# Attention over 16 heads: the products of probabilities and v issued in pairs, in the second and fourth quarter of a step

## The reference

```
# first layer: no mask
attn = softmax(q @ k.T / sqrt(16)) ; out = attn @ v        # 16 heads of 16
x    = layernorm(x + out @ Wo.T + bo)
# second layer: rotary q and k, causal mask, then a mixture of 8 experts (top 2)
h    = x + attention(rmsnorm(x, g1))
x    = layernorm(x + h + moe(rmsnorm(h, g2)))
```

## Time and profile before

| | |
|---|---|
| median of 3 runs | 1528.28 us (1528.12 to 1532.54) |
| profiled execution | 1529.67 us |
| its span, first to last instruction | 1527.9 us |
| granted TensorE clock, mean | 0.923 |
| busy: TensorE, VectorE, ScalarE, GpSimd | 84%, 63%, 54%, 46% of the span |
| `weigh` (L878): 2048 matmuls, busy | 237.2 us |
| attention stage | about 101 to 890 us of the span |

### The profile page before, as it was taken

How to read it: one execution, slowest core, us unless ns; L and a number is a source line. 1 busy time by engine, 2 the same in 40 slices (tenths; PEclk the granted TensorE clock), 3 DMA queues, 4 the chain that set the end, 5 groups by cost and what they waited for, 6 DMA issues and landing times. The chain is left out here.

```text
span 1527.9 us, 33404 instructions
## 1 busy us (share of the span) xinstructions
PE 1283.7 (84%) x11533; PEld 710.7 (47%) x11534; DVE 968.6 (63%) x1778; ACT 829.9 (54%) x1669; POOL 698.7 (46%) x717
## 2 busy tenths in 40 slices
PE   1799999999999999999999831499999999999910
PEld 0222232223223444444443311388888888888810
DVE  6478888888897888787877317443444434444446
ACT  3148888888878777666666620143443334443313
POOL 2324374546455756666564442524443344433312
PEclk9779999999999999999998865599999999999965
DMA  4417576766675878678666438292111111111136
GB/s 122 83 40 169 160 171 177 193 172 180 178 183 170 232 219 222 198 186 225 205 176 163 147 123 238 54 324 70 45 45 45 41 43 46 45 45 41 39 119 222
DMA packets 162442, 212.23 MB, mean 139 GB/s; under 512 B 28576, under 2 KB 124320, under 8 KB 162336
## 3 DMA queue, kind: packets, MB, share of 16 engines
q1 hardware_dynamic: 154848, 190.38, 45.2%
q0 software_dynamic: 7488, 20.46, 4.4%
HBM read 119.55 MB, written 82.58 MB: 132 GB/s over the span
## 5 line engine op out<-in xcount | busy, mean ns | idle before, releaser
L982 ACT ACTIVATE a_probs<-a_ps_s 128x512 f32<-128x512 f32 (+2 forms) x896 | 460.1, 569 | 172.6 <-PE a_ps_s L777 167.3
L1051 DVE TENSOR_REDUCE a_shift_max<-a_ps_m 128x1 f16<-128x512 f32 x512 | 320.7, 684 | 71.0 <-PE a_ps_m L782 69.7
L782 PE MATMUL a_ps_m<-a_qkx 48*128 48x128 f16 (+3 forms) x1408 | 287.0, 304 | 16.9 <-DVE a_shift_max L1051 8.4
L1568 PE MATMUL e_ps_gu<-e_xT,w_up 128*128 128x256 f16 x2574 | 298.1, 274 | 1.5 <-ACT e_xT L1623 1.4
L777 PE MATMUL a_ps_s<-a_qkx 49*128 49x128 f16 (+3 forms) x1408 | 277.9, 298 | 16.5 <-ACT a_probs L982 14.9
L1568 PEld LDWEIGHTS e_ps_gu<-e_xT,w_up 128*128 x2574 | 249.6, 98 | 35.0 <-issue 5.4
L878 PE MATMUL a_ps_o<-a_probs,a_v_one 128*32 128x512 f32 (+3 forms) x2048 | 237.2, 537 | 2.8 <-ACT a_o L989 2.7
L777 PEld LDWEIGHTS a_ps_s<-a_qkx 49*128 49x128 f16 x1408 | 90.7, 95 | 272.8 <-ACT a_probs L982 156.4
L1530 POOL DMA_INDIRECT y<-e_y,e_put x78 | 77.1, 988 | 250.0 <-DVE e_y L1657 238.1
L1668 DVE TENSOR_TENSOR e_h<-e_gate,e_ps_gu 128x512 f32<-128x512 f32 (+2 forms) x156 | 82.7, 551 | 136.8 <-ACT e_gate L1631 119.0
L1590 PE MATMUL e_ps_y<-w_down,e_h 128*128 x1404 | 162.7, 273 | 7.7 <-issue 5.2
(11 more groups left out here) (191 smaller groups left out, 1617.8 us busy)
## 6 DMA issues: line engine op xcount, KB each, us to landing
a_qkx<-a_qk_dram SPq DMA_DIRECT2D x192, 128.0 KB, 4.3
a_qk_dram<-a_qk SPq DMA_DIRECT2D x32, 512.0 KB, 5.5
a_o_dram<-a_o SPq DMA_DIRECT2D x64, 256.0 KB, 2.7
a_o_half<-a_o_dram SPq DMA_DIRECT2D x32, 256.0 KB
a_inv_half<-a_inv_dram SPq DMA_DIRECT2D x32, 256.0 KB
part<-a_part SPq DMA_DIRECT2D x16, 512.0 KB, 5.7
a_q_swap<-a_q SPq DMA_DIRECT2D x64, 128.0 KB, 3.9
c_rows<-y SPq DMA_DIRECT2D x16, 512.0 KB, 5.4
```

The lines of the kernel that those rows point to most:

```text
L782: return pe.matmul(out, qx[first:first + 48, r, pair, q * P:(q + 1) * P], kx[first:first + 48, r, pair, k0:k1], start=start, stop=stop)
L982: act.activation(dst, src, ACT.Exp).then_inc(exp_out, 1)
L1051: vector.tensor_reduce(out, src, AX.X, ALU.max, negate=True).then_inc(max_out, 1)
L1568: mm = pe.matmul(ps_gu[:, bank, kind, f % 2], w[:, ds(e, 1)].rearrange("p o f -> p (o f)"), xT[:, s, xh, k, :], start=n == 0, stop=n == 5)
```

## The change

In place of one `weigh` at the end of each quarter, two stand at the ends of quarters 1 and 3. `kt` 2 and 3 of the step before come together in quarter 1, `kt` 0 and 1 of the present step in quarter 3. Their order among themselves is kept, and the semaphores are those of before.

```
-                    if quarter < 2:
-                        weigh(n - 1, 2 + quarter)
-                    else:
-                        weigh(n, quarter - 2)
+                    if quarter % 2 == 1:
+                        for i in range(2):
+                            weigh(n - (quarter == 1), 2 * (quarter == 1) + i)
```

## The result

The changed kernel takes 1590.84 us, median of 4 runs (1584.28 to 1595.92), against 1528.2 for the kernel before beside it (4 runs): ratio 1.0406, interval 1.0371 to 1.0440, so 62.6 us slower where 49 were forecast. The profiled execution took 1592.98, its span is 1591.3, its mean granted clock 0.916.

A forecast was written before the change was run, and what follows sets the result against it. In unmasked steps VectorE's maxima were taken to bound first halves, and ScalarE's emptying of ps_x nearly to bound second halves, despite TensorE's 95%. Unmasked 42 plus causal 7 gave 49 us on 1528.3: 1577 us, range 1548 to 1606.

The forecast's parts named there:

- Price of a pair: Two weigh in a row on TensorE: 1.00 plus 0.85 us, as the fixed 0.147 is paid once.
- Second half, without a mask: Quarters 2 and 3: the weigh of quarter 2 leaves the wait for ps_x; +0.85 us per step, 3.4 per four-step unit.
- First half, without a mask: Quarters 0 and 1, paced by VectorE's maxima: +0.85, +0.54, +0.79, +0.13 us in steps 13 to 16; 2.31 per unit.
- Step 14's 0.31: Excess in that step's unmasked first half, treated as VectorE backlog that the preceding pair lets it work off; hence +0.54.
- Rival 3: Slower still: clock falls in thinner first halves, 1.5 us more per pair; small form 12 us, 1589; chance 0.14.
- not much thicker: Argument against clock falls: the first stretch's granted clock was 0.99 although its first halves were hardly thicker than the new ones.
- Last eight plain steps: End of the unmasked stretch, with other waits from rotation for the next layer: counted at 1.0 us each.
- Causal steps: The 32 masked steps: about +0.1 us each plus four waits of 0.85; 7 us in sum, bounds -15 and +27.
- The four waits of 0.85 before the output projection: Third step of four of eight causal units: weigh moved behind TensorE's wait before the second output projection, 0.85 us each.
- The range: Whole kernel, 1548 to 1606 us: unmasked steps +27 to +54, causal steps -10 to +20, clock's small form at 1589.
- faster: TensorE sets the pace, so two fewer tiling changes per step save 29 us: 1499, or 1513 causal alone; chance 0.06.
- No difference: ScalarE and VectorE have enough queued to run through a pair, and causal gain and loss cancel: 1528 us; chance 0.06.

The follow-up runs named there:

- e3: Changed kernel with ps_x emptied behind the second exponential or maximum of quarters 2 and 3, not the fourth, in unmasked steps: 1566.93 us, ratio 1.0264 to the kernel before.
- e4: Kernel before with ps_x emptied behind the second exponential or maximum of quarters 2 and 3, not the fourth, in unmasked steps: 1521.99 us, ratio 0.9976.
- e7: Changed kernel plus one unused 512-column reduction on VectorE in quarter 0 of each step with plain maxima: 1635.58 us, one run.
- e8: Kernel before plus one unused 512-column reduction on VectorE in quarter 0 of each step with plain maxima: 1551.14 us, one run.
- e1: Kernel before with only the first half changed: a pair of weigh in quarter 1, single ones kept in quarters 2 and 3: 1565.95 us, ratio 1.0254.
- e5: Changed kernel with each unmasked score product of quarters 0 and 1 issued twice into the same bank: 1591.08 us, ratio 1.0390 to the kernel before.
- e10: Kernel before with the pairs of weigh in the 32 causal steps alone: 1538.78 us, ratio 1.0073.
- e2: Kernel before with only the second half changed: a pair of weigh in quarter 3, single ones kept in quarters 0 and 1: 1554.84 us, ratio 1.0189.

## Why the prediction was right, and where it was off

The sign, the mechanism and the range held: 1590.84 lies in 1548 to 1606, 14 above the 1577.

*Price of a pair.* Right: 1.85 forecast, 1.85 measured. The second `weigh` starts 0.88 behind the first, so the 0.147 is paid once.

*Second half, without a mask.* Right: +0.85 forecast, +0.84 to +0.86 in all four places; 19.4 us over steps 1 to 23 against 23 x 0.85 = 19.6. The second projection starts 2.14 after the scores, 0.06 behind the move out of the bank. How much of the loss that wait is, e3 and e4 show: emptying the bank earlier takes 0.49 off the changed half and 0.07 off the old one. The other 0.37 of the 0.86 is the wait for a score bank, which stands right behind it and which the prediction did not price.

*First half, without a mask.* The mechanism held (e7, e8), a size did not. I took VectorE's pace as 5.01 / 8 = 0.626; that run contained the gap of 0.13, which the `weigh` of quarter 0 had made, and its pace is 0.60. So +0.73 instead of +0.85 in place 1, +0.35 instead of +0.54 in place 2, -0.06 instead of +0.13 in place 0: these three end near 5.8 where I had 5.96. (Step 14's 0.31 was a wait for ScalarE, not for VectorE; the pair ahead of the half takes that away too.) Place 3 has +0.66 for +0.79. Together 1.68 per unit for 2.31. With 3.42 of the second halves a unit costs 5.1 where I had 5.7.

*The clock.* Rival 3 in its small form came on top of the forecast. I had priced a pair at the lower level at 1.5 more and put one per unit, 12 us, at a chance of 0.14. It is 1.54, with six spells over the eight units (seven in the second profile of the changed kernel): 6 x 1.54 = 9 us, of which the kernel before had one spell in its first profile and none in its second. The argument that I set against it, halves "not much thicker" in the kernel before, is the step that failed: one `weigh` less in them took the spells from one or none to six and seven. Before the fall at 421 TensorE was busy 2.32 of 3 us by the window above. In e1, whose halves are the same but for the backlog, it fell twelve times, in e5 once. That forecast and rival 3 together give 1589, so near to 1590.84, is in part luck: the first halves came out 0.63 per unit under the forecast, and the causal steps some 2.5 us over it.

*Last eight plain steps.* Forecast 8, measured 9.2 (12.1 in the second profile), two and three spells among them.

*Causal steps.* Forecast 7, measured 9.5 (7.5 to 15.0) by e10. The composition was as argued: in the two profiles of the changed kernel first halves lose 13 to 16 us over 32 steps, and second ones give back 8 to 11, with spells of the clock in both. How much of the 9.5 is waits and how much clock stays open. The four waits of 0.85 before the output projection I could not see one by one.

*The range.* Its low end was added up wrongly: 27 - 10 = 17 makes 1545, not 1548. Nothing hangs on it.

The rivals: *faster*, by the tiling changes saved, falls. TensorE's busy time for `weigh` did go from 237.2 to 221.4, 16 us saved; plain steps lose them in waits, and in causal ones the second halves get shorter by less than the first ones grow. The rule of the Trainium skill's page "TensorEngine Tiling (Array Packing)", section Key Properties, that a change of mode drains the engine, is not contradicted. The trace agrees that a change costs TensorE something (a pair takes 1.85, two single ones 2.00); in the plain steps that cost was hidden in waits. *No difference* falls as well: ScalarE's idle time ahead of exponentials in the plain stretch went from 68.1 to 118.3 us, VectorE's ahead of maxima from 42.8 to 91.6, by the waits of the kernel before and of the changed one:

```profile
ACT a_probs L982 <- PE a_ps_s L777: 68.1, 97, 2.8
DVE a_shift_max L1051 <- PE a_ps_m L782: 42.8, 85, 2.1
```

```profile
ACT a_probs L981 <- PE a_ps_s L777: 118.3, 124, 4.1
DVE a_shift_max L1050 <- PE a_ps_m L782: 91.6, 106, 2.5
```

Its true core is the backlog: in place 0 the pair indeed costs nothing in the first half.

## What to carry to other kernels

Before you group small pieces of work to save a switch, look at what each piece stands in front of: a piece that fills a wait for a bank or for another engine costs little or nothing where it is, and its switch is hidden with it. An engine that is busy 95% can still be the one that waits; spread its filler, and keep the runs of products between two fillers short: here, with three banks to take them, four score pairs stood between two single `weigh`, and eight between two pairs of them. And when a change leaves an engine that runs at its upper clock less to do between waits, add the price of the lower clock to the forecast itself, not to a rival beside it. The one version that was faster than both kernels, by 0.24% (0.05 to 0.43), keeps the single pieces and empties the shared bank earlier.

## What was not expected of the hardware

First halves that lost one `weigh` of about a microsecond each had up to twelve spells of the lower clock in 31 steps, and products whose result changes nothing kept it (0.93 in e1, 0.97 after, 1.00 in e5). With VectorE, one operation of the same form took 0.68 us and 2.39 us within 3 us of each other; the timelines of e2's VectorE and GpSimd:

```profile
492.92 1.22 DVE L1100 TENSOR_TENSOR a_q_cos<-a_q,rope_cos 128x512 f32<-128x512 f32 x1
...
661.49 0.68 DVE L1100 TENSOR_TENSOR a_q_cos<-a_q,rope_cos 128x512 f32<-128x512 f32 x1
...
664.35 2.39 DVE L1100 TENSOR_TENSOR a_q_cos<-a_q,rope_cos 128x512 f32<-128x512 f32 x1
```

```profile
492.82 0.77 POOL L610 CAST a_w_part<-a_w_in 128x704 f16<-128x704 f32 x1
...
661.55 1.09 POOL L551 CAST a_aT<-a_o_half 128x512 f16<-128x512 f32 x1
...
663.83 2.35 POOL L598 TENSOR_TENSOR a_x_res<-a_hid,a_x_res 128x1024 f32<-128x1024 f32 x1
```

The slow one starts inside a GpSimd operation with two inputs and ends 0.56 behind it (666.74 and 666.18). The fast one starts 0.06 ahead of the conversion beside it, so it does not show that a conversion, with its one input, lets VectorE pass: the operation at 492.92 starts inside one and ends 0.55 behind it (494.14 and 493.59). The fourteen traces together have 448 VectorE operations of this tile and form. In 431 of them the length is, to 0.06, the larger of two values: 0.68, or what the GpSimd operation running at the start still takes, plus 0.55. Of the other 17, eleven stand beside GpSimd operations of 128x4, and six start within 0.03 of GpSimd's. The Trainium skill's page "GPSIMD Engine Reference", section Specifications, says that GpSimd shares its way to the on-chip memory with VectorE and contends with VectorE's operations that have two inputs there; these rows agree. No run here tested it by itself.
